# A 2-D spectral tower on one core: the column transform with the data as stationary operand, its modes copied by ScalarE, column frequencies paired in the mix, and layer 0 in the hardware loop

## The reference, cut to what matters

```python
def _spectral_conv(x, w):                      # x: images, 32 channels, 64, 64
    x_ft = jnp.fft.rfft2(x, norm='ortho')
    out = jnp.einsum('bixy,ioxy->boxy', x_ft[:, :, :20, :20], w)
    out_ft = zeros.at[:, :, :20, :20].set(out)
    return jnp.fft.irfft2(out_ft, s=(64, 64), norm='ortho')
x = coords @ fc0_w + fc0_b
for sw, cw, cb in four layers:
    x = gelu(_spectral_conv(x, sw) + einsum('bchw,oc->bohw', x, cw) + cb)
```

## Time and profile before

| | |
|---|---|
| median of three runs | 1547.61 us |
| the profiled execution, its own time | 1544.01 us |
| its span | 1542.2 us |
| TensorE busy, matmuls | 1369.6 us, 89% |
| VectorE busy | 1181.8 us, 77% |
| ScalarE busy | 532.8 us, 35% |
| granted TensorE clock, mean over the span | 0.988 of full speed |

### The profile page before, as it was taken

How to read it: one execution, slowest core, us unless ns; L and a number is a source line. 1 busy time by engine, 2 the same in 40 slices (tenths; PEclk the granted TensorE clock), 3 DMA queues, 4 the chain that set the end, 5 groups by cost and what they waited for, 6 DMA issues and landing times. The chain is left out here.

```text
span 1542.2 us, 69028 instructions
## 1 busy us (share of the span) xinstructions
PE 1369.6 (89%) x32216; PEld 704.4 (46%) x32216; DVE 1181.8 (77%) x1433; ACT 532.8 (35%) x673; POOL 92.4 (6%) x45
## 2 busy tenths in 40 slices
PE   8888999997999999879999998778779998989996
PEld 3544444445444444544444445445531117853332
DVE  4499999997999999789999997555510007878886
ACT  2422222223222222222222222333359994421221
POOL 1000000000000000000000000000000000036551
PEclk9999999999999999999999999999999999999998
DMA  6324242346666666566666663899997751056420
GB/s 230 115 115 164 116 163 119 133 166 224 249 247 244 249 241 255 177 255 246 245 245 245 245 250 130 311 372 387 375 377 278 280 190 59 8 129 152 116 76 14
DMA packets 59934, 315.80 MB, mean 205 GB/s; under 512 B 16704, under 2 KB 18688, under 8 KB 25984
## 3 DMA queue, kind: packets, MB, share of 16 engines
q1 hardware_dynamic: 36512, 177.95, 34.0%
q10 hardware_dynamic: 23264, 135.49, 21.4%
HBM read 176.05 MB, written 137.36 MB: 203 GB/s over the span
## 5 line engine op out<-in xcount | busy, mean ns | idle before, releaser
L890 ACT ACTIVATE act_c<-slots,conv_b 128x1024 f32<-128x1024 f32 x256 | 282.1, 1115 | 717.8 <-PE slots L579 717.8
L776 DVE STREAM_TRANSPOSE inv_out<-slots 128x1024 f32<-128x1024 f32 x256 | 304.7, 1229 | 96.7 <-PE slots L541 96.7
L579 PEld LDWEIGHTS slots<-inv_w,inv_out 64*64 64x64 f32 x16384 | 270.7, 136 | 198.9 <-issue 188.7
L579 PE MATMUL slots<-inv_w,inv_out 64*64 64x64 f32 x16384 | 301.6, 224 | 14.7 <-issue 9.6
L752 DVE STREAM_TRANSPOSE turned_h<-slots 128x1024 f32<-128x1024 f32 x200 | 238.0, 1229 | 24.5 <-PE slots L474 24.4
L474 PE MATMUL slots<-turned_w,fwd_w 32*64 32x512 f32 x3200 | 201.5, 599 | 28.7 <-DVE inv_out L776 22.1
L741 DVE STREAM_TRANSPOSE turned_w<-act_c 128x1024 f32<-128x1024 f32 x192 | 225.6, 1218 | 0.8 <-ACTq L893 0.8
L541 PE MATMUL slots<-turned_k,inv_h 64*64 64x320 f32 x2048 | 169.3, 444 | 53.7 <-DVE turned_h L752 30.4
L563 PE MATMUL slots<-xin,conv_w 32*32 32x512 f32 x3072 | 112.7, 605 | 29.3 <-DMA xin<-act_scratch 17.6
L486 PE MATMUL slots<-turned_h,fwd_h 64*64 64x320 f32 x1600 | 132.7, 443 | 1.3 <-DVE turned_h L752 1.3
L541 PEld LDWEIGHTS slots<-turned_k,inv_h 64*64 64x64 f32 x2048 | 71.0, 133 | 131.1 <-DVE turned_h L752 76.5
(11 more groups left out here) (166 smaller groups left out, 1116.8 us busy)
## 6 DMA issues: line engine op xcount, KB each, us to landing
act_scratch<-act_c ACTq DMA_DIRECT2D x128, 1024.0 KB, 4.2
xin<-act_scratch SPq DMA_DIRECT2D x96, 1024.0 KB, 4.8
act_c<-act_scratch SPq DMA_DIRECT2D x32, 1024.0 KB, 6.1
mode_w<-in_sw_dram SPq DMA_DIRECT2D x20, 640.0 KB, 4.3
at_turned<-level_scratch SPq DMA_DIRECT2D x24, 256.0 KB, 4.2
at_ret_t<-level_scratch SPq DMA_DIRECT2D x20, 256.0 KB, 4.2
xin<-in_x_dram SPq DMA_DIRECT2D x4, 1024.0 KB, 8.6
turned_w<-in_x_turned_dram SPq DMA_DIRECT2D x3, 1024.0 KB, 5.4
```

Of the source, the lines that this page charges most:

```text
L579: mm = nc.tensor.matmul(banks[half * 64:(half + 1) * 64, 2 * two + odd, at:at + 64], inv_out[rows, t % 2, i, two, s, 2 * half:2 * half + 2 ...
L776: nc.vector.transpose(dst, src).then_inc(inv_turned, 1)
L890: nc.scalar.activation(act_c[:, t % RING, :, at, :].rearrange("p i q m -> p q i m"), banks[:, at, :].rearrange("p q (i m) -> p q i m", i=2 ...
```

## The change

The column transform over h (`dft_h`) swaps its operands. The turned data is now the stationary operand (128 rows, 64 columns: the two parts of h stand in one contraction), and the constants move past it, 40 elements a time. There are 20 matmuls for a pair in the place of 8. Their result lies as `modes` wants it, and so a plain copy of 128x400 by ScalarE (`copy_modes`) replaces VectorE's transpose of 128x640; at the front VectorE copies (`copy_first`). `inverse_h` contracts 32 rows in the place of 64, in 16 matmuls of the same 320 moving elements. In `dft_w` the output places are exchanged. The order of the column frequencies in `modes` is new, and with it the halves that `mix` writes to. Layer 0 goes into the loop; its input comes for each pair by four transfers of 32 KB, and its convolution reads 4 rows in each block of 32. `lift` has two matmuls of 64 rows and columns for each pair.

```diff
+        def mix_place(u, side):
+            block, odd = (2 * (u // 4) + side, u // 2 % 2) if u < 8 else (4, side)
+            return 2 * block + odd
+        def modes_from(at):
+            return banks[:, at:at + 2, 0:200].rearrange("p i (k x) -> p i k x", x=MODES)
+            def load_x(t):
+                if t >= IN_RING:
+                    sp.wait_ge(summed, after_out(0, t - IN_RING, 0))
+                for p in range(4):
+                    sp.dma_start(flat(xin[p * CH:p * CH + IN_CH, t % IN_RING]), x[t, p]).then_inc(
+                        xin_in[t % IN_RING], 16)
...
@@ dft_w
-                            mm = nc.tensor.matmul(banks[i * 64:(i + 1) * 64, 4 + p, :],
+                            g = i ^ p % 2
+                            mm = nc.tensor.matmul(banks[g * 64:(g + 1) * 64, 4 + 2 * i + p // 2, :],
@@ dft_h
-                for ph in range(2):
-                    take(w_turned, after_w_turned(n, ph))
-                    for i in range(2):
+                for i in range(2):
+                    take(w_turned, after_w_turned(n, i))
+                    for b in range(MIXES // 2):
                         for kwh in range(2):
-                            mm = nc.tensor.matmul(banks[kwh * 64:(kwh + 1) * 64, at + i, 0:320],
-                                                  fwd_h[i * 64:(i + 1) * 64, parity, ph, :],
-                                                  turned_h[i * 64:(i + 1) * 64, n % 2, ph,
-                                                           kwh * 320:(kwh + 1) * 320].rearrange(
-                                                      "p (b c m) -> p b m c", c=CH, m=2),
-                                                  start=(ph == 0), stop=(ph == 1))
+                            at_kw = kwh * 320 + b * 64
+                            mm = nc.tensor.matmul(
+                                banks[kwh * 64:(kwh + 1) * 64, at + i, b * 40:(b + 1) * 40],
+                                turned_h[:, n % 2, i, at_kw:at_kw + 64],
+                                fwd_h[:, i, parity, :].rearrange("p (k x) -> p k x", k=2)[:, :, 0:MODES],
+                                start=(b == 0), stop=True, skip_group_check=True)
                 mm.then_inc(h_done, 1)
...
@@ mix
-                                to = kwh ^ side
+                                k, kh = mix_place(u, side), u % 2 * 5 + m
+                                to = kwh ^ k // 2 % 2
@@ inverse_h
-                for i in range(2):
+                for odd in range(2):
                     for s in range(2):
-                        for kwh in range(2):
-                            rows = slice(kwh * 64, (kwh + 1) * 64)
-                            mm = nc.tensor.matmul(banks[s * 64:(s + 1) * 64, 4 + 2 * i + kwh, 0:320],
-                                                  inv_h[rows, l % 2, s * 64:(s + 1) * 64],
-                                                  turned_k[rows, t % 2, i * 320:(i + 1) * 320],
-                                                  start=True, stop=True)
+                        for r in range(4):
+                            rows = slice(r * 32, (r + 1) * 32)
+                            mm = nc.tensor.matmul(
+                                banks[s * 64:(s + 1) * 64, 4 + r, :].rearrange("p (i n) -> p i n", i=2)[:, :, 0:160],
+                                inv_h[rows, l % 2, odd, s * 64:(s + 1) * 64],
+                                turned_k[rows, t % 2, odd * 320:(odd + 1) * 320].rearrange("p (i n) -> p i n", i=2),
+                                start=(odd == 0), stop=(odd == 1))
@@ conv, layer 0
-                        w = first_w[rows_p, t % LIFT_E, :] if l == 0 else conv_w[rows_p, l, :]
+                        rows_p = slice(p * 32, p * 32 + (IN_CH if l == 0 else CH))
+                        w = first_w[rows_p, :] if l == 0 else conv_w[rows_p, l, :]
...
@@ steps, and the order of a layer
-                used = [(act_high, 2), (inv_turned, 4), (modes_turned, 2), (act_in[0], 16), (act_in[1], 16)]
+                inputs, size = (xin_in, 64) if l == 0 else (act_in, 16)
+                used = [(act_high, 2), (inv_turned, 4), (modes_turned, 2), (inputs[0], size), (inputs[1], size)]
-                looped = 2 * ((PAIRS - 1 - first) // 2) if l > 0 else 0
+                looped = 2 * ((PAIRS - 1 - first) // 2)
...
@@ VectorE: turn_h is gone from every step and from the end of a layer
-                    if 3 <= j < PAIRS - 1:
-                        turn_h(forward(l + 1, j - 3), modes[:, 2 * (j - 3):2 * (j - 3) + 2])
@@ ScalarE
+            def copy_modes(f, t, at=0):
+                act.wait_ge(h_done, forward(f, t) + 1)
+                nc.scalar.copy(modes[:, 2 * t:2 * t + 2, :, 0:MODES], modes_from(at)).then_inc(modes_set, 1)
...
                     act.drain().then_inc(act_ready, 1)
+                    if t >= 3 and l < LAYERS - 1:
+                        copy_modes(l + 1, t - 3)
                     act.dma_start(act_dram[t], flat(act_c[:, t % RING])).then_inc(act_stored[t % RING], 16)
+                if l < LAYERS - 1:
+                    for t in range(PAIRS - 3, PAIRS):
+                        copy_modes(l + 1, t, at=0 if t == PAIRS - 2 else 2)
```

More of the change, by code:

```diff
@@ L91, in dft_constants @@
                     inv_h[parity, :, kh % 2, at + 1, p % 2, 1, n] = cos[h, kh]
+    full_h = np.zeros((2, 2, 2, 16, 2, 2, 2, 32))
+    for g in range(2):
+        for i in range(2):
+            part = slice(16 * (g ^ i), 16 * (g ^ i) + 16)
+            full_h[g, :, :, :, i] = fwd_h[:, 0, :, part].transpose(1, 3, 2, 0, 4, 5)
+    whole_h = np.zeros((4, 32, 2, 2, 128))
+    for b in range(4):
+        whole_h[b] = inv_h.reshape(2, 2, 2, 32, 128)[:, 0].transpose(2, 0, 1, 3)
     kw = np.arange(MODES)
-    place, kwh = kw % MIXES, kw // MIXES
-    places = 16 * (kwh ^ place % 2) + place
+    kwh, b, m = kw // MIXES, kw % MIXES // 2, kw % 2
+    places = 8 * (2 * (kwh ^ b % 2) + m) + b
     inv_w = np.zeros((2, 2, 32, WW))
@@ L412, in _ @@
                 load_mode_w(0, pair)
-            for q in range(2):
-                sp.dma_start(flat(xin[:, q]), x[q]).then_inc(xin_in[q], 16)
+            for t in range(IN_RING):
+                load_x(t)
             for l in range(LAYERS):
@@ L501, in lift @@
                     pe.wait_ge(first_w_set, 1)
-                for b in range(4):
-                    rows_b = slice(b * 32, (b + 1) * 32)
-                    mm = nc.tensor.matmul(banks[rows_b, 2 + n % 2, 0:400], lift_w[rows_b, e, :],
-                                          in_modes[rows_b, 2 * q:2 * q + 2, :, 0:MODES], start=True, stop=True)
+                for kwh in range(2):
+                    rows = slice(kwh * 64, (kwh + 1) * 64)
+                    mm = nc.tensor.matmul(banks[rows, 2 + n % 2, 0:400], lift_w[rows, e, :],
+                                          in_modes[rows, 2 * q:2 * q + 2, :, 0:MODES], start=True, stop=True)
                 mm.then_inc(lifted, 1)
@@ L568, in keep_busy @@
                 for _ in range(n):
-                    nc.tensor.matmul(banks[:, b, 384:512], inv_h[:, 0, :], inv_h[:, 0, :], start=True, stop=True)
+                    nc.tensor.matmul(banks[:, b, 384:512], inv_h[:, 0, 0, :], inv_h[:, 0, 0, :], start=True, stop=True)
             def inverse_w(l, t, two):
@@ L602, in step @@
                         take(inv_turned, after_inv_turned(l, j + 1, 1))
+                    else:
+                        take(w_turned, after_w_turned(forward(l + 1, j - 3), 1))
                     dft_w(forward(l + 1, j - 2))
@@ L629, in _ @@
             pe.wait_ge(fc0_cols_set, 1)
-            for e in range(LIFT_E):
-                mm = nc.tensor.matmul(banks[:, 3, e * CH:(e + 1) * CH], fc0_cols[:, e, :], conv_w[0:CH, 0, :],
-                                      start=True, stop=True)
-            mm.then_inc(first_w_filled, 1)
+            nc.tensor.matmul(banks[:, 3, 0:CH], fc0_cols, conv_w[0:CH, 0, :],
+                             start=True, stop=True).then_inc(first_w_filled, 1)
             warm_up(1)
@@ L661, in _ @@
                 first = 1 if last else 4
-                looped = 2 * ((PAIRS - 1 - first) // 2) if l > 0 else 0
+                looped = 2 * ((PAIRS - 1 - first) // 2)
                 for j in range(1, first):
                     step(l, j)
-                if looped:
-                    steps(l, first, looped)
+                steps(l, first, looped)
                 for j in range(first + looped, PAIRS):
@@ L714, in _ @@
             for _ in range(4):
-                nc.tensor.matmul(banks[:, 0, 0:128], inv_h[:, 0, :], inv_h[:, 0, :], start=True, stop=True)
+                nc.tensor.matmul(banks[:, 0, 0:128], inv_h[:, 0, 0, :], inv_h[:, 0, 0, :], start=True, stop=True)
         def mix_part(u, side, images=slice(0, IMAGES)):
-            k, half = u // 2 * 2 + side, u % 2
+            k, half = mix_place(u, side), u % 2
             dst = modes[:, images, k, half * 10:half * 10 + 10].rearrange("p i (m r) -> p i m r", r=2)
@@ L828, in _ @@
```

(10 more changed lines are left out.)

92 lines of the change are left out of this document (44 added, 48 removed).

## The result

The changed kernel takes 1617.04 us in the median of four runs (1615.01 to 1619.91), the kernel before, run beside it, 1549.98 (1542.99 to 1553.77): a ratio of 1.0439, with an interval of 1.0395 to 1.0483, and 67 us more. The forecast was 1590 and the range ended at 1614, so the side was right and the size was not: 42 us were forecast, and the result lies 3 us outside the range.

A forecast was written before the change was run, and what follows sets the result against it. It took the turn of banks 4 to 7, not VectorE, to set the step. Terms 5.6 + 18.2 + 9.5 + 9.0 - 1.0 + 1.0 gave +42.3 us, 1590 us as a median, range 1560 to 1614.

The forecast's parts named there:

- The ring of banks 4 to 7: In a usual step, `inverse_h`, `turn_inverse`, `dft_w` and `turn_w` follow each other at once and set its 8.41 us.
- Rival A: VectorE was the bound after all: usual steps fall by some 0.4 us, 1534 us in all; chance 0.06.
- `dft_h`, usual step: Column transform in a usual step: 40 passes in 20 rounds take 1.35 us against 1.31, and the later end is hidden.
- Rival C: Weight loads aren't hidden: `dft_h` takes 0.6 us longer, 44 us more in all, 1634 us; chance 0.08.
- `inverse_h`: In each step of layers 0 to 2 it takes 0.06 us more, unhidden: +5.6 us.
- rival D: Row tiles sharing a bank take turns in `dft_w`: +158 us, 1748 us; chance 0.02.
- The back-edge: At the loop's end in layers 1 and 2, TensorE's count-down starts 0.70 us later in 26 steps: +18.2 us.
- Rival B: TensorE's queue holds `dft_h`, so the loop's end grows by 0.2 to 0.36 us only: 1574 us; chance 0.17.
- Layer 0 in the loop: Layer 0 gains its 3.1 us of instruction fetch stalls but pays 12.6 us for 13 loop ends: net +9.5 us.
- three stalls of 3.1 us in all: Instruction fetch waits in unrolled layer 0, between 95 and 315 us, that putting it in the loop would save.
- The mix: Two of ten steps use two of four tiles, +1.12 us each, the others as before: +9.0 us over four layers.

## Why the prediction was wrong in size

*What bounds the kernel.* Right. The ring of banks 4 to 7 is what sets a step: the usual step came out at 8.47, as forecast, `turn_inverse` waits in every step for `inverse_h`, and relieving VectorE changed 8.41 into 8.41. Rival A is gone.

*`dft_h`, usual step.* Right: 1.36 us against 1.35, hidden. Rival C is gone with it. The Trainium skill (TensorE: Matmul & The Clock Gate, "The mechanism") says that a weight load overlaps a matmul in flight only where the two differ in their row group, and here all use all rows. By that rule the section would have taken some 1.9 us, by the estimate of rival C; 20 rounds of two column tiles took 1.36, so the trace disagrees.

*`inverse_h`.* Right in the ring (1.34 for 1.31, and 0.06 a step by the experiment). What I missed is that it takes more behind some back-edges: 0.2 us in layer 1, 0.1 in layer 0, nothing in layer 2.

*`dft_w`.* 1.98 us, unchanged: rival D is gone. The Trainium skill (TensorEngine Tiling (Array Packing), "Gotcha 1: PSUM Pressure") says that different row tiles can't access one bank at once; two of them in each bank cost no time here, as four cost none in the earlier trace rows. In both kernels, though, row tiles that share a bank write different rows of it, so no run shows what happens where they write the same ones.

*The back-edge.* The mechanism was right and the size too small. `inverse_h` starts 1.01 us late against 0.27 before, 0.74 more, where I had taken 0.70. To this come 0.16 for the slower `inverse_h` (L804 starts 1.60 after it and not 1.44), which makes 0.90 in layer 1; layer 2, where `inverse_h` isn't slower and most of these steps take 9.44 to 9.49, shows 0.75. That is 13 x 0.90 + 13 x 0.75 = 21.5 us in place of 18.2. Rival B, a queue that holds all of `dft_h`, is gone: 18 of its 40 loads were still to start when the count-down began.

*Layer 0 in the loop.* The step that failed is "three stalls of 3.1 us in all" against 13 back-edges of 0.97. The back-edges cost 1.06 each, 13.8 us. The three stalls went, as forecast, but two steps before the loop repeats took 10.41 and 10.17 us. The kernel before had one such step, 10.48, which the prediction's window from 95 on left out. The 10.41 is for the most part the clock (0.51 from 84.2 to 91.1). In the three kernels that set `to = kwh ^ side`, where layer 0's steps are the same code, these two took 8.47 to 8.48 and 8.63 us, so this part is not the same in every execution. Forecast 11 with `inverse_h`, measured 14.8.

*The mix.* Two steps on two tiles: right, 2.16 and 2.19 against 2.3. That the other eight are "as before" was wrong. I had compared which tiles a step writes and not which addresses they read together. The sum came out near (10.4 for 9.0) by luck: against a mix without waits it would have been 17, and the slower steps hide the waits that the mixes before had.

*The first steps of layers 1 and 2: no term at all.* This is the largest miss, and the step of the prediction that failed most. I had counted instruction fetch for layer 0 only the earlier trace rows, and taken for granted that the layers whose code runs through four unrolled steps and once through the loop before it repeats go on as they were. But a step now has 264 passes where it had 224, and each is a load and a matmul. Over 8.47 us a step, the back-edge's part taken off, layer 1 lost 0.46 + 1.76 + 1.93 + 3.70 + 1.11 = 9.0 us in five steps and layer 2 1.32 + 1.49 + 1.55 + 2.17 = 6.5 in four, where the kernel before lost 0.7 in both together: 15 us more. With the count-downs early 7.4 of the 9.0 stayed, so it is not the back-edge. The three kernels that set `to = kwh ^ side` show the same bursts, 11.7 to 13.3 us in the longest step of each. A part of it is the clock behind a wait and no wait itself: in the step of 13.32 us `inverse_h` alone lost 1.17 us to it.

Added up, the misses are 15 in these steps, 3.3 at the back-edges of layers 1 and 2, 3.7 in layer 0, 1.4 in the mixes, 1.5 in layer 3, and 7.1 in the front and in the last stage, which the change hardly touches or not at all: 32 of the 33.6 us between 42.3 and 75.9. Against the medians the miss is 25, since the profiled execution of the changed kernel is 2.9 above its median and that of before 6.0 below the 1549.98 that it is compared with.

What isn't settled is where the next burst falls, and what makes it. That TensorE waits for code there is a reading and not shown: it rests on the waits for issue and the slow sections, the blocks on the instruction queue at the same time, and the smaller bursts with 16 or 24 passes fewer in a step. No experiment kept the passes and changed the fetch alone.

## What to carry to other kernels

Where a loop's end makes one engine's queue do work, price what stands before it in instructions, not in microseconds: a section of many short matmuls delays all that the queue has to do behind it, and counting semaphores down a section earlier, as soon as their last waiter is through, gave 45 us here for no work at all. An engine without idle time need not be the bound; look at what starts right after what, and only then at the busy shares. And where a rewrite takes more instructions for the same columns, look at the steps before a loop repeats as well: here they cost 15 us in two layers, and less with 16 or 24 passes fewer in a step.

## What I had not expected of the hardware

Two column tiles that work at the same time slow each other by the distance of what they read: 40 passes of 128 elements took 1.46 us with 256 or 512 bytes between the two sides' places, and 1.10 or 1.26 with 128 or 640.

A matmul group behind nine count-downs and a branch of TensorE's queue can be slow itself: 32 passes took 1.56 us in layer 1, 1.45 in layer 0 and 1.34 in layer 2, where elsewhere they take 1.34; 16 passes took 1.31 in all three.

Behind a wait of 1.06 us, and around a late back-edge of 1.42, the granted clock was 0.57 for eight microseconds: the step got 4.8 us longer than a usual one, more than the two waits together. Such waits alone don't say when it falls. The kernel before waited 1.74, 1.04 and 1.41 us between 76 and 92 us, and its granted clock there was 1.00. With `inverse_h` as before the clock was 0.50 for 3.4 us three times in layer 0's loop (from 119.6, 174.2 and 228.9 us on), behind back-edges like all the others, and each time a usual step took 9.45 to 9.52 us.
